# Causal attention block on one core: where the last pair of heads is turned when a wide query step is followed by a narrow one

## The reference, cut to what matters

```python
c_Q = rms_norm(x @ Wq_down, q_norm_w)
q_nop = (c_Q @ Wq_up).reshape(B, T, N_HEAD, NOPE_DIM)
q_pe = (c_Q @ Wq_pe).reshape(B, T, N_HEAD, ROPE_DIM)      # then rotated
...
scores = jnp.einsum('bhqd,bhkd->bhqk', q, k) * SCALE
scores = jnp.where(mask[None, None], scores, jnp.finfo(scores.dtype).min)
attn = jax.nn.softmax(scores, axis=-1)
y = jnp.einsum('bhqk,bhkd->bhqd', attn, v)
y = y.transpose(0, 2, 1, 3).reshape(B, T, N_HEAD * V_DIM)
return y @ Wo
```

## Time and profile before

| | |
|---|---|
| time, three runs | 1768.68 us median, 1767.13 to 1769.35 |
| the profiled execution | 1769.41 us |
| its span, first to last instruction | 1767.6 us, mean granted TensorE clock 0.992 |
| busy: TensorE, VectorE, ScalarE, GpSimd | 1689.5, 1335.2, 1135.4, 585.8 us |
| transposes F to FT, QS to Q | 348 and 128 issues, all from SyncE's queue |
| DMA traffic | 255.05 MB, mean 144 GB/s |

### The profile page before, as it was taken

How to read it: one execution, slowest core, us unless ns; L and a number is a source line. 1 busy time by engine, 2 the same in 40 slices (tenths; PEclk the granted TensorE clock), 3 DMA queues, 4 the chain that set the end, 5 groups by cost and what they waited for, 6 DMA issues and landing times.

```text
span 1767.6 us, 29331 instructions
## 1 busy us (share of the span) xinstructions
PE 1689.5 (96%) x9200; PEld 849.7 (48%) x9200; DVE 1335.2 (76%) x3369; ACT 1135.4 (64%) x2463; POOL 585.8 (33%) x1042
## 2 busy tenths in 40 slices
PE   3589999999999999999999999999999999999998
PEld 3445555444544445545454455544454444554443
DVE  5688887777788687777868687876878868777765
ACT  5677676656667566666656566666756656666663
POOL 1223333333334233333323333333333323333320
PEclk9899999999999999999999999999999999999999
DMA  9338977878978787986879878786897877897786
GB/s 262 83 70 146 153 136 145 152 130 151 156 131 156 136 151 143 161 154 119 157 121 164 163 135 149 143 148 120 155 151 142 153 128 150 147 156 146 138 153 120
DMA packets 911877, 255.05 MB, mean 144 GB/s; under 512 B 897384, under 2 KB 899946, under 8 KB 911338
## 3 DMA queue, kind: packets, MB, share of 16 engines
q1 hardware_dynamic: 902336, 235.29, 74.7%
q10 hardware_dynamic: 8938, 15.80, 3.3%
q0 software_dynamic: 448, 2.10, 0.6%
HBM read 20.32 MB, written 8.39 MB: 16 GB/s over the span
## 4 chain that ended last, share of the span: by engine, by line
PE 75%; issue 7%; DVE 6%; ACT 4%; DMA 4%; POOL 2%; SPq 1%; ACTq 0%; DVEq 0%; POOLq 0%
PE bank L581 6%; PE bank L582 6%; PE bank L584 6%; PE bank L583 6%; PE bank L613 5%; PE bank L631 5%; PE bank L633 5%; PE bank L632 5%; PE bank L615 5%; PE bank L614 5%; PE bank L593 3%; DVE F L1307 2%; DMA XT<-XS 2%; ACT P L893 2%; PE bank L586 2%
## 5 line engine op out<-in xcount | busy, mean ns | idle before, releaser
L893 ACT ACTIVATE P<-P,nm 128x512 f32<-128x512 f32 (+7 forms) x512 | 395.0, 772 | 458.2 <-DVE nm L1293 455.7
L1293 DVE CUSTOM_DVE_ANT_0 P<-bank,mask,neg 128x512 f32<-128x512 f32 (+7 forms) x512 | 402.9, 815 | 288.3 <-PE bank L593 167.8
L1503 POOL TENSOR_SCALAR sn<-sm 128x1 f32<-128x1 f32 x512 | 208.2, 407 | 950.7 <-ACT P L893 941.7
L888 ACT ACTIVATE F<-P,rc 128x512 f16<-128x512 f32 (+7 forms) x512 | 384.0, 767 | 98.2 <-DVE rc L1301 80.1
L1307 DVE SCALAR_TENSOR_TENSOR F<-P,rc,F 128x512 f16<-128x512 f32 (+7 forms) x512 | 413.0, 820 | 2.8 <-ACT F L888 2.4
L581 PE MATMUL bank<-K,Q 128*128 128x512 f16 (+3 forms) x760 | 248.6, 327 | 8.4 <-DMA Q<-QS 8.4
L582 PE MATMUL bank<-K,Q 128*128 128x512 f16 (+3 forms) x760 | 248.5, 327 | 0.0
L584 PE MATMUL bank<-K,Q 128*128 128x512 f16 (+3 forms) x760 | 248.5, 327 | 0.0
L583 PE MATMUL bank<-K,Q 128*128 128x512 f16 (+3 forms) x760 | 248.5, 327 | 0.0
L613 PE MATMUL bank<-FT,V 128*128 128x512 f16 x568 | 216.7, 382 | 3.3 <-DVE WO L1335 3.3
L614 PE MATMUL bank<-FT,V 128*128 128x512 f16 x568 | 215.5, 379 | 0.0
(11 more groups left out here) (210 smaller groups left out, 2658.0 us busy)
## 6 DMA issues: line engine op xcount, KB each, us to landing
out<-X ACTq DMA_DIRECT2D x31, 256.0 KB, 3.7
X<-in_x ACTq DMA_DIRECT2D x28, 256.0 KB, 3.3
FT<-F SPq DMA_TRANSPOSE x348, 4.2
wo<-in_Wo SPq DMA_DIRECT2D x4, 1024.0 KB, 9.3
V<-CC SPq DMA_DIRECT2D x32, 64.0 KB, 2.6
Q<-QS SPq DMA_TRANSPOSE x128, 4.0
X<-in_x SPq DMA_DIRECT2D x4, 256.0 KB, 7.5
ua<-in_Wq_up SPq DMA_DIRECT2D x1, 1024.0 KB, 11.2
```

Source lines behind the costliest of these rows:

```text
L888: return e.eng.activation(dst, src, ACT.Copy, scale=scale)
L893: e.eng.activation(m.P[:, u % 4, 0:w], m.P[:, u % 4, 0:w], ACT.Exp, bias=m.nm[:, u % 8:u % 8 + 1], scale=-1.0, accum_out=m.sm[:, u % 8:u % ...
L1293: e.eng.tensor_tensor_reduce(out=m.P[:, u % 4, 0:w], in0=m.pS[u % 2][:, off:off + w], in1=m.mask[:, 1024 - w:1024], scale=m.neg[:, :], sca ...
```

## The change

Of an early step only the last pair is now turned in its own half step; the first pair goes behind, into the second half step. At the nine places (`joined(n)`) the queries of step n + 4 are turned between the two pairs of the wide step, not after both; ScalarE writes YH of step n between the two high halves of the last pair, and VectorE writes YL between the two low halves, in step n itself, where before it was written in step n + 1 after the two maxima. At the end of the kernel the last pair of step 126 is also turned in its own half step (there without `joined`), and YH of step 124 goes behind both of that pair's high halves.

```diff
-def early(n):
-    return halved(where(n)[1]) and (n == N - 1 or not halved(where(n + 1)[1]))
+def early(u):
+    n = u // 4
+    return n == N - 1 or (u % 4 >= 2 and halved(where(n)[1]) and (n == N - 2 or not halved(where(n + 1)[1])))
+
+
+def joined(n):
+    return n + AHEAD < N - 2 and early(4 * (n + AHEAD) + 3)
...
                 scaled_hi(u)
-                if p and not early(n + AHEAD):
+                if p and not early(u) or p and joined(n):
                     values_hi(n)
                 scaled_hi(u + 1)
-            if p and (u >= 4 * N or early(n + AHEAD)):
+            if p and (u >= 4 * N or early(u)) and not joined(n):
                 values_hi(n)
...
-            if p == 0 and n and first:
+            if p == 0 and n and first and not joined(n - 1):
                 values_lo(n - 1)
             if u < 4 * N:
                 maximum(u)
                 maximum(u + 1)
-            if p == 0 and n and not first:
+            if p == 0 and n and not first and not joined(n - 1):
                 values_lo(n - 1)
...
-            behind = u < 4 * N and not early((u - 1) // 4)
+            behind = u < 4 * N and not early(u - 1)
...
-            if u < 4 * N and early(u // 4):
+            if u < 4 * N and early(u):
                 scaled_lo(u)
+                if p and joined(n):
+                    values_lo(n)
                 scaled_lo(u + 1)
...
-            if p == 0 and n + AHEAD + 1 < N:
+            if p == 0 and n + AHEAD + 1 < N and not (n and joined(n - 1)):
                 turn_queries(n + AHEAD + 1)
-            if u < 4 * N and not early((u - 1) // 4):
+            if u < 4 * N and not early(u - 1):
                 turn_probabilities(u - 2)
                 turn_probabilities(u - 1)
-            if u < 4 * N and early(u // 4):
+            if p and joined(n):
+                turn_queries(n + 2 * AHEAD)
+            if u < 4 * N and early(u):
                 turn_probabilities(u)
                 turn_probabilities(u + 1)
```

## The result

The changed kernel took 1777.66 us, the median of ten runs (1771.64 to 1781.01), beside 1769.43 for ten of the kernel before: ratio 1.0047, interval 1.0035 to 1.0059. It is 0.47% slower. The forecast was 1762.3 us, with a range up to 1768. One execution further down, the profiled one of e7, took 2538.8 us at a granted clock of 0.656 and is left out of the ratios.

The account below looks back on a forecast made before the run. TensorE, busy 96%, was taken as the bound, with 18.7 of its 23.6 us of waits aimed at. Gains of 5.7 (C), 0.7 (A and B) and 0 (end), 6.4 us, took 1768.7 to 1762.3 us, range 1757.0 to 1768.0.

Parts of the forecast that it names:

- A and B: Places n = 21, 53, 85 (A) and 29, 61, 93 (B): 0.7 us to win in all, capped by XT's landing.
- The same five transposes end at about the time at which they ended before: SyncE's queue, u0 to u3 and Q: reordered, u3 lands at 581.6 to 583.4 at n = 37; backlog ended at 583.5 before.
- The forecast's own caution: Skill page: ScalarE's loads share the 16 DMA engines with SyncE's transposes, which speaks against a gain from mere reordering.
- YL earlier: At the nine places, YL written in step n ends the wait in `combine`: worth 10.3 us if nothing is late next.
- The first pair behind: Two low halves move to the second half step, covered by VectorE's idle time: cost 0, 0.3 us a place on the bad side.
- Q before u2 and u3: In SyncE's queue Q takes u2's turn, ending its 8.4 us of waits; u2 and u3 go one turn later each.
- C: Places n = 37, 69 and 101: 1.9 us won at each, 5.7 in all, bounds 4.8 to 7.0.
- XT behind them: XT's time in SyncE's queue is not moved, capping gains: 2.5 us at n = 37, at most 0.4 at A and B.
- The end: From step 126's last pair to the wait for FTL: gain taken as 0, ends -0.7 to +0.7 us.
- rival 1: The wait for Q becomes one for u3: C wins 1.9 us, A and B nothing, 1766.8 us; chance 0.25.
- Rival 3: VectorE's maxima come late in the narrow step after each place: slower, 1774 us; chance 0.09.
- Rival 2: The transposes' backlog gets shorter, XT comes forward and caps rise: 1756 us, or 1750.0 with everything gone; chance 0.12.

Follow-up runs that it names:

- e7: e2 with ScalarE's load of X one half step earlier: 1766.74 us, ratio 0.9994.
- e3: The whole change at the three places C only, the rest as in the kernel before: 1766.40 us, ratio 0.9977.
- e2: The kernel before with only the queries turned between the two pairs at the nine places: 1762.91 us, ratio 0.9963.
- e11: e2 with the load of X one half step later: 1761.23 us, ratio 0.9961.
- e6: e2 with YL and YH written between the parts of the last pair, both pairs in their own half step: 1767.07 us, ratio 0.9994.
- e12: e6 with the load of X one half step later: 1765.03 us, ratio 0.9977.
- e5: The changed kernel with YL and YH back at their old places: 1770.12 us, ratio 1.0015.
- e10: e1 with the load of X one half step later: 1775.72 us, ratio 1.0039.
- e4: The whole changed kernel with the load of X one half step later: 1765.97 us, ratio 0.9979.
- e9: The kernel before with only the load of X moved ahead of ScalarE's copies of the queries in the same half step: 1778.30 us, ratio 1.0053.
- e1: The changed kernel with the queries turned after all four units again, as before: 1798.07 us, ratio 1.0152.
- e8: The changed kernel with 12 more matmuls in front of the weighing at A and B: 1774.16 us, ratio 1.0034.

## Why the prediction was wrong

The table has, for the six places A and B, how far behind the issue of the last of five the load of X is issued (smallest and largest), how long that transpose takes to land and when it lands after the issue of u0 (both us, means over the six), and at how many of the six the clock fell. All is worked out from the rows of each kernel.

| kernel | load behind | takes | lands | falls | ratio |
|---|---|---|---|---|---|
| before | 2.0 to 2.7 | 4.2 | 13.1 | 0 | 1 |
| e3 (A, B as before) | 2.1 to 3.0 | 4.3 | 13.1 | 0 | 0.9977 |
| e2 queue | 2.4 to 3.0 | 4.4 | 13.1 | 0 | 0.9963 |
| e11 queue, load late | none there | 4.7 | 13.3 | 0 | 0.9961 |
| e6 queue, YL | 1.5 to 2.1 | 4.9 | 13.6 | 2 | 0.9994 |
| e12 queue, YL, load late | none there | 5.0 | 13.8 | 1 | 0.9977 |
| e5 queue, first pair | 0.7 to 2.2 | 5.0 | 13.9 | 1 | 1.0015 |
| e10 rest, load late | none there | 4.7 | 14.0 | 3 | 1.0039 |
| e4 all, load late | none there | 5.3 | 14.1 | 1 | 0.9979 |
| e9 before, load earlier | -0.2 to 1.2 | 5.3 | 14.2 | 1 | 1.0053 |
| e1 rest | 0.6 to 1.5 | 6.2 | 15.1 | 5 | 1.0152 |
| after | 0.4 to 1.8 | 6.1 | 15.2 | 4 | 1.0047 |
| e8 after, 12 matmuls more | 0.2 to 1.7 | 6.4 | 15.3 | 1 | 1.0034 |

**The step that failed** is "The same five transposes end at about the time at which they ended before", and with it "all that stands before it in the queue is the same work", on which the term of A and B rests: -0.7 us forecast, +13.1 measured. The queue's list is the same work, but it isn't alone on the 16 DMA engines. I had read SyncE's queue only, and never asked what the other queue does as soon as TensorE is no longer held. With YL's wait gone (1.47 us at A, 0.90 at B) ScalarE runs forward too, the load of X 1.6 us at A and 1.3 at B against u0, and these 256 KB start 0.4 to 1.8 us behind the last issue in place of 2.0 to 2.7. That transpose then takes 6.1 us in place of 4.2, and lands 2.1 us later. YL isn't alone in bringing the load forward: the first pair, moved behind, does it by 0.8 to 0.9 us by itself (e5). e4, by the load alone, takes 11.7 us away, 11.4 of them at A and B. In the landings that is 1.1 of the 2.1 us, 6.7 us over six places; most of the rest is gone with three of the four falls of the clock. The other 1.0 us of the landings stays. e9, by the load alone, loses 9.3 us of time but 6.2 at A and B, where the change lost 13.1: most of the loss needs the load, and the load isn't all of it.

The forecast's own caution was the right rule and I gave it too little. The Trainium skill, "DMA: Bandwidth & Descriptors", section "Issuing engines are not separate DMA queues", says that loads issued by another engine share the same 16 DMA engines; e9 agrees, 9.3 us for a load moved by 1.8 to 3.0 us. I used it against a gain from reordering, and not to ask whether a load would move.

**YL earlier: the mechanism right, the worth wrong.** YL is written at 363.15 and `combine` starts at 364.65 without a wait at n = 21, and the waits fell from 12 to 3 as said. But the 10.3 us were to be won only where nothing is late next, and the last tile of FT is late next, everywhere: e11 against e12, 10.3 us less for YL and 11.7 more for FT. By the ratios YL costs 5.5 us in e6 against e2; there it is 2.8, which noise could make. The forecast had capped the gain of A and B at 0.7 us; that it could turn into a loss there, it didn't ask.

**The first pair behind, costed at 0,** costs 9.2 us between e2 and e5 (0.9963 to 1.0015), and 9.4 between e6 and the whole change (0.9994 to 1.0047). The next maxima weren't late, as said, and u0 was issued on time but for 0.2 us at the places B. It acts through the load too, at least with YL moved: with the load late, e12 against e4, no cost is seen (0.9977 to 0.9979).

**Q before u2 and u3: right.** The waits for Q are gone, and e2 alone wins 6.5 us of the 8.4, the most of any part. At C u3 was issued at 577.6 (forecast 577.1 to 578.3) and `weigh` began at 583.6 (forecast 583.2). C gave 5.2 us in place of 5.7; the term that is off is the landing, 5.8 us at n = 37 in place of 4.5 to 5.1. TensorE waited 1.2 to 1.4 us for FT there, where 0.3 to 1 was forecast. C loses little to the load: it is 1.8 to 2.1 us behind the last issue, near to where it was (2.0 to 2.3).

**XT behind them: right in its time, idle as a cap.** XT is issued at 371.35 at n = 21 (371.22 before), and behind u0 within 0.5 us of before at all of A and B but n = 93, where it is 1.0 later. But TensorE waits for it nowhere, since it waits longer for u3 just before: the forecast 4 to 9 us of new waits "and L373 for XT at most of A and B" are 23.8 us for FT alone.

**The clock was in no term.** Waits of 3.3 to 3.9 us, where the longest of before was 2.2, brought four stretches of some 3.3 us at 1.2 GHz. At these four places the kernel lost more than its waits grew by: 1.2, 1.5, 1.3 and 1.3 us (n = 21, 29, 53, 85), 5.3 in all; at the two others of A and B, with no fall, it lost 0.3 less than they grew by. TensorE's busy time, 5.7 us longer, agrees. So by this estimate some 5 of the 13.1 us are the clock's. The waits themselves are 23.8 less 3.7 at C, 20.1 us, in place of 11.6: YL 7.1, Q 8.4 - 1.5 - 1.5 - 2.2 = 3.2 and XT 1.3. That is 8.5 more; with 5.3 for the clock and less 0.6 at n = 61 and 93 it makes the 13.1.

**The end** gave about 0 as said: the wait for FTL is 2.0 against 2.1. **The rivals:** rival 1 had the right kind of wait, "The wait for Q only becomes one for u3", and no way to be longer than what it replaced. Rival 3 named the right sign for a reason that didn't occur: no wait of L587 for a maximum stands in the trace. Rival 2, a backlog that gets shorter, is wrong in sign. **The bounds:** the forecast's own end of 1765.0 doesn't add up. Its terms give 4.8 + 0 - 0.7 = 4.1 us, 1764.6, and with data late by 0.3 us at nine places 1767.3.

**What stays open.** The load doesn't explain all. With no load in the way the last of five lands at 14.1 in e4, 13.8 in e12, 13.3 in e11: with YL moved it is later by 0.5 us, with the first pair too by 0.8, and the places wait for it. ScalarE's store of the output starts 0.9 to 1.0 us sooner behind u0 wherever the first pair is behind (e4, and after), but not in e12, so it can't be the reason for the 0.5; whether it is for the rest was not tried. Nor is it settled why a load that starts earlier (e7) costs less than the one of e9, or why the cost at one place differs so from another. The kernel before with the load late was not run; e11 against e2 stands in for it.

## What to carry to other kernels

When a wait goes, list the transfers of every queue that the engines issue behind it, not only the queue under study: they come forward by about the time won, and one that then falls just behind a transfer that is waited for can cost more than the wait did. Where a stretch is bound by transfers, as here, an earlier engine won nothing; what wins is to put the transfer that is waited for first ahead (e2: 6.5 us of 8.4), and to keep large loads that nobody needs soon out of that stretch. Split a change into its parts before keeping it: here one part won 6.5 us and the rest lost 15.

## What the runs showed of the hardware

- A load of 256 KB by ScalarE's queue, issued 0.4 us behind a DMA transpose of SyncE's queue, was seen with landings of 5.5 and 5.7 us for that transpose (e9 and after, n = 21), against 4.4 with 2.0 us between the two issues; at n = 29 of e9 with 4.7, against 3.8 with 2.5 us between them. Here a transfer that was issued later took time from one that was issued before it.
- The issue of the delayed transpose hardly shows this: at n = 21 it takes 1.81 us after and 1.70 before. The issue behind it does, 2.78 against 1.68, though it begins within 0.13 us of its old time. The landing shows it in full.
- Behind waits of 3.33 to 3.87 us TensorE's granted clock was 0.51 to 0.63 for some 3.3 us. Behind waits of 2.69 and 2.82 (n = 61 and 93 of the kernel after) it stayed at 1.00, but a wait of 2.54 in e4 at n = 21 was followed by 0.54 (below), and the clock also fell behind the waits of 2.15 and 2.05 of e6 (n = 21 and 53), so the length of the wait alone doesn't tell it.

```profile
374.90:378.30 3.40, 3.39 (x12) 1.56 (x13) 0.00 (x0) 0.00 (x0) 0.00 (x0) 0.54 0.58 120
```
